# Rebuilding the self-attention stage of a fused perceiver layer

## The reference

```
x = x + xattn(layernorm(x), ctx, ...)          # 16 heads of 32, rope, softmax, @ W_o + b_o
x = x + attn(layernorm(x), w_qkv, w_o, log_scale)
x = x + ffn(layernorm(x), router, experts, shared expert)

def attn(x, w_qkv, w_o, log_scale):
    q, k, v = split(x @ w_qkv)                 # 16 heads of 32
    q, k = rotate(q, cos, sin), rotate(k, cos, sin)      # theta = pos * INV_FREQ * exp(log_scale)
    scores = einsum('bhqd,bhkd->bhqk', q, k) / sqrt(32)  # causal mask
    out = softmax(scores) @ v
    return out @ w_o
```

## Time and profile before

| | |
|---|---|
| median of 3 runs | 1686.07 us (1685.53 to 1690.05) |
| profiled execution | 1690.07 us |
| its span (first to last instruction) | 1688.8 us |
| mean granted TensorE clock | 0.961 |
| busy share PE, PEld, DVE, ACT, POOL | 95%, 58%, 70%, 64%, 38% |
| first output product, first projection, first score | 1170.22, 1195.64, 1261.91 |
| last values end, router's first product | 1346.9, 1371.74 |

### The profile page before, as it was taken

The page is one execution under the profiler, slowest core; times in us unless marked ns, Lnnn a source line. Parts: engine busy times, 40 slices in busy tenths (PEclk is TensorE's granted clock), DMA queues, the critical chain, the costliest instruction groups (busy, mean ns, idle before and its releaser), DMA issues. The chain is left out here.

```text
span 1688.8 us, 25470 instructions
## 1 busy us (share of the span) xinstructions
PE 1606.0 (95%) x9520; PEld 973.1 (58%) x9520; DVE 1186.3 (70%) x2784; ACT 1075.5 (64%) x1276; POOL 649.2 (38%) x357
## 2 busy tenths in 40 slices
PE   8899999999998699999999999998979789999998
PEld 6666666666665444444443443445745468888886
DVE  6888887888778679999989998997842442222222
ACT  5478777777787588888888888886312433333331
POOL 0289988788889213111221210000200124444441
PEclk9999999999999899999999999999955989999999
DMA  5534533433350585445554444552010014343441
GB/s 191 174 138 149 189 138 115 174 138 138 117 196 27 175 211 136 116 112 125 125 125 107 119 125 108 124 124 86 28 56 1 1 33 150 127 126 127 128 129 49
DMA packets 88162, 200.83 MB, mean 119 GB/s; under 512 B 8863, under 2 KB 9128, under 8 KB 85734
## 3 DMA queue, kind: packets, MB, share of 16 engines
q1 hardware_dynamic: 88000, 199.15, 39.6%
q10 hardware_dynamic: 38, 0.05, 0.0%
HBM read 143.48 MB, written 55.65 MB: 118 GB/s over the span
## 5 line engine op out<-in xcount | busy, mean ns | idle before, releaser
L771 ACT ACTIVATE P<-PS 128x1024 f32<-128x1024 f32 x512 | 480.5, 1038 | 86.7 <-PE PS L765 83.4
L788 DVE TENSOR_TENSOR acc<-acc,P 128x2048 f32<-128x2048 f32 x216 | 498.5, 2368 | 32.4 <-ACT P L771 32.1
L473 DVE CUSTOM_DVE_ANT_0 rel<-PS,rel 128x256 f32<-128x256 f32 x1024 | 363.2, 421 | 104.9 <-PE PS L460 100.4
L466 ACT ACTIVATE rel<-PS 128x1024 f32<-128x1024 f32 x256 | 263.3, 1028 | 111.8 <-PE PS L460 110.4
L797 PE MATMUL PS<-P,qe 128*32 128x512 f32 x2048 | 257.0, 600 | 0.7 <-ACT on L802 0.7
L108 POOL TENSOR_TENSOR El<-We,Eh 128x1536 fp32r<-128x1536 f32 x36 | 126.2, 3505 | 166.2 <-ACT Eh L105 166.1
L114 PE MATMUL PS<-Wh,R 128*128 128x512 f32 x512 | 184.2, 422 | 1.0 <-ACT kr L656 0.9
L114 PE MATMUL PS<-R,Eh 128*128 128x512 f32 x576 | 182.1, 397 | 3.0 <-POOL El L108 3.0
L114 PE MATMUL PS<-R,Wh 128*128 128x512 f32 x512 | 172.9, 409 | 0.8 <-ACT kr L656 0.8
L1234 DVE TENSOR_TENSOR hf<-sg,PS 128x512 f32<-128x512 f32 x36 | 24.7, 687 | 192.6 <-PE PS L114 189.4
L460 PE MATMUL PS<-khd,qh 32*128 32x256 f32 x2048 | 131.9, 331 | 21.1 <-ACT rel L466 11.3
(11 more groups left out here) (236 smaller groups left out, 2408.5 us busy)
## 6 DMA issues: line engine op xcount, KB each, us to landing
khd<-kscr SPq DMA_DIRECT2D x129, 256.0 KB, 4.2
We<-in_w_e SPq DMA_DIRECT2D x36, 768.0 KB, 5.8
y<-in_y SPq DMA_DIRECT2D x16, 1024.0 KB, 4.9
vscr<-vo SPq DMA_DIRECT2D x16, 1024.0 KB, 4.9
kscr<-khd SPq DMA_DIRECT2D x16, 1024.0 KB, 7.1
kscr<-kl SPq DMA_DIRECT2D x16, 1024.0 KB, 5.9
qe<-vscr SPq DMA_DIRECT2D x64, 256.0 KB, 2.7
kl<-kscr SPq DMA_DIRECT2D x63, 256.0 KB, 4.1
```

Source lines behind the costliest of these rows:

```text
L466: return AC.sig(nc.scalar.activation(rel[i][:, :, :, :], PS[:, 2 * b:2 * b + 2, :].rearrange("p j (t n) -> p j t n", t=2), ACT.Relu))
L473: m = DV.sig(nc.vector.tensor_tensor_reduce(out=rel[i][:, j, t, :], in0=PS[:, 2 * b + j, t * 256:(t + 1) * 256], in1=rel[i][:, j, t, :], s ...
L771: expm[s, pr] = spfree[b] = AC.sig(nc.scalar.activation(P[s % 4][:, 2 * pr:2 * pr + 2, :], PS[:, 2 * b:2 * b + 2, :], ACT.Exp, scale=SCALE))
L788: accm[s] = DV.sig(nc.vector.tensor_tensor(a[:, :, :], a[:, :, :], P[s % 4][:, :, :], ALU.add))
```

## The change

Cross-attention side: the loads of the q and k weights go to step 200 of its loop, into the buffers `W0` that now serve as the sums of groups 0 and 2; the absolute value of the angles goes to step 232; the bias of the output product is added to X on GpSimd at steps 129 to 141; the output parts of a group are made later and with one instruction of ScalarE and one of VectorE. The warm-up products and the square-root table load ahead of the barrier go.

Self-attention: the output products of groups 0 to 2 are issued ahead of the last group's, in both places; the normalization works on pairs of tiles; q and k are projected for groups 0 and 1 first and for groups 2 and 3 inside the head loop; the maxima of a group are computed in the group before it; the scores are one fp32 product per head on the whole q and k, for two heads at a time.

```diff
@@ end of the cross-attention @@
         AC.wait(PL.last(), t_eps)
-        m = AC.sig(nc.scalar.activation(cs2[:, 0, :, :], cs2[:, 1, :, :], ACT.Abs))
+        m = t_abs[0]
...
-        AC.sig(nc.scalar.activation(rstd[:, 0:1], epst[:, 0:1], ACT.Sqrt))
         denominators(3)
-        dfree, t_ot = outputs(3)
         PE.wait(expm[total - 1, 0], expm[total - 1, 1])
-        warm(26, 0)
         barrier()
@@ output products and normalization @@
+        def norm_tiles(o, ready, xn, hT, lT, fill):
+            done = []
+            for p_ in range(2):
+                for qt in (2 * p_, 2 * p_ + 1):
+                    DV.wait(ready[qt])
+                    m_ = DV.sig(nc.vector.tensor_tensor(X[:, qt, :], X[:, qt, :], o[qt], ALU.add))
...
+                m_ = AC.sig(nc.scalar.activation(r_, mv[:, 2 * p_:2 * p_ + 2, 1], ACT.Sqrt, bias=epst[:, 0:1]))
...
+                for qt in (2 * p_, 2 * p_ + 1):
+                    m_ = DV.sig(nc.vector.tensor_scalar(xn[:, qt, :], X[:, qt, :], mv[:, qt, 0:1], rstd[:, qt:qt + 1],
+                                                        ALU.subtract, ALU.mult))
+                    fill(qt)
+                    done.append(transpose_tile(xn, hT, lT, qt, m_))
+        for qt in range(4):
+            out_products(qt, PS[:, qt, :], (0, 1, 2), True, False)
+        PE.wait(a, t_o3)
+        t_out1 = [PE.sig(out_products(qt, PS[:, qt, :], (3,), False, True)) for qt in range(4)]
+        DV.wait(m_qw)
+        t_qws = DV.sig(nc.vector.tensor_tensor(wl[0][:, :, :], W0[0][:, :, :], wh[0][:, :, :].bitcast(F32), ALU.subtract))
+        t_kws = low_parts(1, W0[1], m_kw)
+        t_xT = norm_tiles([PS[:, qt, :] for qt in range(4)], t_out1, xn2, R[0], R[1], lambda t: warm(5, 4 + t))
@@ scores(g, j) becomes scores(g, j, hp) @@
-            for i, (kp_, qp_) in enumerate(((0, 0), (1, 0), (0, 1))):
-                for hd in range(4):
-                    nc.tensor.matmul(o[hd], QK[1][kp_][rows[hd], g, j * 128:(j + 1) * 128],
-                                     QK[0][qp_][rows[hd], g, 128 * j:512], start=i == 0, stop=False)
+            for i, hd in enumerate(heads):
+                nc.tensor.matmul(o[i], qk[1][rows[hd], g, j * 128:(j + 1) * 128], qk[0][rows[hd], g, 128 * j:512],
+                                 start=True, stop=False)
@@ the loop over groups @@
+        for qt in (3, 2, 1, 0):
+            for hp in range(2):
+                row_maxima(0, qt, hp)
+                run(fill, 3)
+        run(fill)
...
         for g in range(4):
+            fill = itertools.chain.from_iterable(projection(p_, g + 2) for p_ in range(2) if g < 2)
+            run(fill, 6)
+            shifts(g)
+            run(fill, 3)
...
+            for i, (j, hp) in enumerate(sc_):
+                scores(g, j, hp)
+                if mx:
+                    row_maxima(g + 1, *mx.pop(0))
+                run(fill, 2)
+                if i % 2 and j:
+                    values(g, j - 1)
+            run(fill)
+            values(g, 3)
+            if g < 2:
+                high(0, g + 2)
+                high(1, g + 2)
+            weighted(g)
+            if g == 1:
+                for g_ in range(2):
+                    attention_parts(g_)
...
             if g == 2:
+                attention_parts(2)
                 t_rws = split(rw[:, :, :], rwh[:, :, :], rwl[:, :, :], t_rw)
```

More of the change, by code:

```diff
@@ new lines, in build @@
+        m = DV.sig(nc.vector.reciprocal(rec3[:, :], DEN))
+        DV.wait(m)
+        m = DV.sig(nc.vector.tensor_tensor(o3[:, :], o3[:, :], rec3[:, :], ALU.mult))
+        AC.wait(qw["in"])
+        m_qw = AC.sig(nc.scalar.copy(wh[0][:, :, :], W0[0][:, :, :]))
+        AC.wait(m)
+        a = AC.sig(nc.scalar.activation(R[0][:, 3, :], o3[:, :], ACT.Identity, bias=cst[:, 19:20]))
+        m_kw = AC.sig(nc.scalar.copy(wh[1][:, :, :], W0[1][:, :, :]))
+        AC.sig(nc.scalar.activation(dmy[:, 0:1], epst[:, 0:1], ACT.Sqrt))
@@ L921, in build @@
+        SP.wait(t_qws)
+        t_wo = lane("l_o").dma(SP, W0[0][:, :, :], A["w_o"].rearrange("(k p) n -> p k n", p=128))
+        for e in range(3):
+            l_e[e].dma(SP, W[e][:, :], A["w_e"][e])
         AC.wait(t_const)
@@ L1055, in build @@
-        t_at, oc_free, t_wos = {}, {}, []
-        def values(n):
-            g, j = bursts[n]
+            PE.wait(t_nmz[g], pairfree[b])
+            heads = (2 * hp, 2 * hp + 1)
+            o = [PS[:, 2 * b + i, 0:w] for i in range(2)]
+            for i, hd in enumerate(heads):
+                nc.tensor.matmul(o[i], qk[1][rows[hd], g, j * 128:(j + 1) * 128], qk[0][rows[hd], g, 128 * j:512],
+                                 start=True, stop=False)
+            for i, hd in enumerate(heads):
+                nc.tensor.matmul(o[i], onr[rows[hd], :], nmz[g % 2][rows[hd], 128 * j:512], start=False, stop=False)
@@ L1059, in values @@
+            for i in range(2):
+                ins = nc.tensor.matmul(o[i][:, 0:128], idr[:, :], mkr[:, 128:256], start=False, stop=True)
+            st_use[g] = m_ = PE.sig(ins)
+            AC.wait(m_, pfree.get(n - 2))
+            pairfree[b] = ex2[n, hp] = AC.sig(nc.scalar.activation(
+                Pt[n % 2][:, 2 * hp:2 * hp + 2, 0:w], PS[:, 2 * b:2 * b + 2, 0:w], ACT.Exp))
+        t_at, oc_free = {}, {}
+        def values(g, j):
+            n = 4 * g + j
             w = 512 - 128 * j
-            PE.wait(ex2[n], oc_free.get(g - 1), pairfree[3])
+            PE.wait(ex2[n, 0], ex2[n, 1], oc_free.get(g - 1), evq[2, j])
@@ new lines, in build, with attention_parts, run @@
+        t_as = {}
+        def attention_parts(g):
+            t_as[g] = split(at_[:, g, :], R[0][:, g, :], R[1][:, g, :], t_at[g], [kdone[2, 3], kdone[0, 3], kdone[1, 3]])
+        def run(steps, n=None):
+            for _ in itertools.islice(steps, n):
+                pass
+        for u in range(2):
+            run(projection(0, u))
+        for u in range(2):
+            run(projection(1, u))
+            high(0, u)
+        high(1, 0)
+        fill = itertools.chain.from_iterable(projection(2, u) for u in range(4))
```

361 lines of the change are left out of this document (178 added, 183 removed).

## The result

The changed kernel takes 1700.7 us in the median of four runs (1699.13 to 1712.09), beside 1685.8 us for the kernel before in the same comparison: a ratio of 1.0100 over all executions, 95% interval [1.0060, 1.0141] (the two medians alone give 1.0088). That is slower by some 15 us. The forecast was 1704.0, in the range 1674 to 1732, with 0.65 on slower.

What follows compares the result with a forecast made beforehand. It took TensorE to be the bound in most of the stage, with its clock and pauses deciding. Terms summed to -10.2 us at 2.4 GHz, low clock added 28: net +18, 1708 profiled, 1704 median, range 1674 to 1732.

Steps and rivals of the forecast that it cites:

- end of the cross-attention: Before the barrier: ScalarE's sines follow the copy at once and end at 1166.7 instead of 1170.0, -3.3 us.
- output products, normalization, clock up to the first score: First normalization as two pairs of 9.1 us on VectorE, 27.6 us for 25.4: +2.2, plus low clock there.
- projection to first score: First projection to first score: 66.3 us falls to 31.2 as projections and maxima move and the 7 us pause goes, -35.1.
- four groups: The four head groups: 85.0 us grows to 108.2 at 2.4 GHz through half bursts and new waits, +23.2, plus low clock.
- the lower of the two bounds: First normalization: q's low part on VectorE beside GpSimd's k part costs 0, with 4 us as the upper bound.
- price of a half burst: Scores in the groups: two heads at 512 columns take 1.65 us at 2.4 GHz; all widths 10.5 us a group.
- pairs of fp32 products do not overlap: Rival, scores: two fp32 products on two row groups run one behind the other, +17 us, about 1722; chance 0.10.
- The waits: Ahead of groups 1, 2 and 3: TensorE idles 2.9, 7.1 and 6.5 us for the shift copy queued on ScalarE.
- the clock in group 2: Group 2: half clock behind the wait until the 512-column values, costing 8 us.
- main case: Groups 1 to 3: clock falls at the waits and rises at each group's 512-column values; 1692 to 1718, chance 0.42.
- low to the end: Rival, clock: no rise inside groups 1 to 3, 47 us in place of 22.5, about 1728; chance 0.13.
- the low stretches are begun by pauses: Whole stage: TensorE's clock drops to 0.50 behind pauses; low clock priced at +28 us in all.

Runs made afterwards that it cites:

- e_four: a_early with the fp32 scores of all four heads in one burst instead of two half bursts; 1679.3 us, ratio 0.9965 to the kernel before.
- a_early: Changed kernel with the next group's shift issued ahead of the last values, and casts and the output weights' high part moved into the next group; 1676.4 us, ratio 0.9968.
- a_warm: Changed kernel with 10, 30 and 28 small fp32 products filling TensorE's waits ahead of groups 1, 2 and 3; 1691.0 us, ratio 1.0049.
- b_warm: The kernel before with 30 small fp32 products in its 6.5 us pause behind the second maxima; 1672.0 us, ratio 0.9934.
- a_quad: Changed kernel with the normalization on all four tiles at once instead of pairs; 1697.7 us, ratio 1.0083.
- e_dense: a_early with two small fp32 full-array products ahead of each half burst of groups 2 and 3; 1679.9 us, ratio 0.9980.
- e_best: a_early plus bursts of four heads, normalization on four tiles and 14 warm-up products ahead of the barrier; 1667.9 us, ratio 0.9909.
- e_half: e_best with half bursts of two heads again in place of its bursts of four; 1671.2 us, ratio 0.9913.
- e_mixed: e_half with bursts of four heads in groups 2 and 3, half bursts kept in groups 0 and 1; 1658.6 us, ratio 0.9844.
- a_three: Changed kernel with three fp32r products on the high parts for each fp32 score product, lower accuracy; 1701.3 us, ratio 1.0121.

## Why the prediction was right, and where it was off

The terms, in us, for the profiled executions (spans 1688.8 and 1710.8):

| term | predicted, clock included | measured |
|---|---|---|
| end of the cross-attention | -3.3 | -4.35 (first output product 1170.22 to 1165.87) |
| output products, normalization, clock up to the first score | +2.2, +4 | +3.87 |
| projection to first score | -35.1 | -35.27 |
| four groups | +23.2, +22.5 | +52.46 |
| tail | +2.8, +1.5 | +3.35 |
| expert stage | 0 | +1.94 |
| sum | +17.8 | +22.0 |

**Barrier.** ScalarE's sines end at 1165.77, where 1166.7 was predicted; 0.9 of the difference is work that came in earlier from the cross-attention (the copy ends at 1160.57, before at 1161.48).

**Normalization.** Two pairs, from 1176.61 to the second pair's start at 1185.49, 8.9 us, and from there to the end of the last low part at 1195.01, 9.5 us, the second partly at half clock: right. The low part of q on VectorE took 2.28 us and had no visible price, the lower of the two bounds, but only its last 1.0 us lay beside GpSimd's work. By the Trainium skill ("GPSIMD Engine Reference", Specifications) it could have waited as in the earlier trace rows. The term was +3.9, not +6 with clock on top. Such a wait is there elsewhere in this kernel: beside GpSimd's low parts of the v weights a VectorE product of the rotation (L1011, at 1200.45) took 1.78 us where it takes 0.68 by itself; TensorE was busy meanwhile, so it cost nothing.

**First projection to first score.** 31.0 against 31.2, at clock 1.00. It is the gain of the change and it is all there.

**The groups.** The price of a half burst, 1.65, came out as forecast, in part by luck: fp32 and shift products took 1.28 where 0.86 + 0.23 = 1.09 stood in the sum, and the rest 0.37 where 0.79 - 0.23 = 0.56 did. The rival that pairs of fp32 products do not overlap falls: in e_four four of them took what two do, which agrees with the Trainium skill ("TensorE: Matmul & The Clock Gate", Part 3) on row groups. The waits were 2.35, 6.69 and 5.59 where 2.9, 7.1 and 6.5 were predicted, and a_early shows that the order on ScalarE made them: without them 1.3% is gone. Group by group, score to score: predicted 31.2, 42.3, 36.2, 21.0; measured 29.96, 42.48, 43.18, 21.82.

**The step that was mis-sized** is the clock in group 2: 8 us in the sum, 15 in the profiled run (43.18 less the 28.2 of the sum at 2.4 GHz). The prediction let the clock rise at the values of 512 columns of each group, as it had in the earlier trace rows. In group 1 it did (values at 1274.35, 0.50 until 1278.5, and once more for 3.8 us from 1282.3, with TensorE never idle) and in group 3 (values from 1352.93, rise at 1357.2). In group 2 the same values ran at 1314.89 and the clock stayed at 0.50:

```profile
1258.30:1278.50 20.20, 20.20 (x64) 9.39 (x66) 7.01 (x9) 3.85 (x5) 2.83 (x3) 0.50 0.00 1
1278.50:1296.00 17.50, 13.41 (x107) 7.70 (x103) 7.55 (x10) 5.28 (x10) 0.00 (x0) 0.89 0.00 1
1296.00:1357.20 61.20, 53.01 (x218) 26.67 (x218) 14.21 (x16) 12.77 (x19) 0.00 (x0) 0.50 0.00 0
```

So the run was the main case in groups 1 and 3 and the rival "low to the end" in group 2. In the other executions, with a higher mean clock, some 10 us are not lost, wherever they lie.

**How much of the hit is luck.** The groups were 6.8 us and the expert stage 1.9 us longer than forecast; barrier, normalization and tail were 4.3 us shorter, and so the sum missed by 4.2 only. The forecast of 1704 was the profiled 1708 less the 4 us by which the profiled run of the kernel before lay over its median; here that distance was 11.4. The median lies 3.3 us under the forecast and the profiled run 4.1 us over it: direction and mechanism were right, the last few us are not evidence for the terms.

**A premise that does not hold as written:** that the low stretches are begun by pauses. The trace of before already spoke against it. The prediction says that the old groups 2 and 3 held 1.00, but group 2 began at 1318.50 and the row at 1326.00; in between the clock fell behind a wait of 1.32 us, with TensorE busy in the low stretch itself:

```profile
1322.80:1325.80 3.00, 3.00 (x23) 1.93 (x20) 2.20 (x2) 0.67 (x2) 0.00 (x0) 0.50 0.03 5
```

And a_warm, a_early and b_warm have low stretches in which TensorE is busy for all or nine tenths of the time, and each of them gained less than this premise gave (by the ratios 9 of 29, 22 of 38, 11 of 28 us). The pauses explain the idle time and part of the low clock.

**What was not foreseen:** the expert stage took 319.00 us against 317.06, at a clock of 0.83 in its first 20 us against 0.91. Of the ten kernels of the experiments, six take 317.0 to 317.1 there (b_warm, a_quad, e_dense, e_best, e_half, e_mixed), a_three 318.5, and e_four, a_early and a_warm 319.3 to 320.9, though none of them changes that stage; why is open.

**What stays open** is what in the bursts brings the clock down when TensorE is busy. Products on 32 rows stand in each of the long low stretches, while the first projections kept 1.00 in every kernel; but the same products ran at 1.00 through group 0 of the change (29.96 us) and group 3 of e_half; more full-array products (e_dense) and fuller bursts (e_mixed) both shortened the low stretches. No run here separates rows in use, size of product and share of time.

## What to carry to other kernels

An in-order engine turns its order into waits: a copy of 0.6 us that another engine needs next must not stand behind long work that nobody there waits for, such as a cast that waits for a reciprocal; here three such places (two behind a reciprocal, one behind a cast of 1.89 us) cost 22 us in 1700, more than the change had lost. Split a burst only for a reason that a row shows: a burst of two heads cost nearly what a burst of four did, and with a third pair of banks bursts of four were 12 us faster than half bursts, while with two pairs they waited and gained nothing. And price a product at both clocks, and say for each stretch at which it will run; a stretch with many small products can lose the clock with no pause at all.

## What the runs showed of the hardware

- The granted clock stood at 0.50 for 30.00 us with TensorE busy for 29.25 of them (a_early) and for 14 us with no idle time at all (a_warm, 0.52 over the stretch). The Trainium skill ("TensorE: Matmul & The Clock Gate", Part 1) has the clock follow how busy the engine has been; with busy time as the profile counts it, these stretches do not agree.
- Unbroken work did not always bring it back: behind the wait of 6.69 us the clock stayed at 0.50 from 1298.60 to 1335.70 with TensorE busy for all 37.10 us (after).
- Filling a pause with small products moved the fall of the clock and shortened the low stretch, but did not prevent it: in b_warm it fell at 1244 in place of 1230.8 and was low for 31 us in place of 77.6.
- At 2.4 GHz and 512 columns, fp32 products of 32 rows with their shift products take 1.30 us on four row groups (e_four) and 1.28 on two (after), from the first start to the start of the mask products; three fp32r products in place of each fp32 one, on two row groups, take 1.13 with the shift (a_three). The two parts cannot be told apart by their starts: the same shift products take 0.72 behind fp32 products and 0.33 behind fp32r ones.
- VectorE beside GpSimd can wait: 1.78 us for a product that takes 0.68 by itself (after, 1200.45).
